# Window attention in a fused two-block kernel: the addition of the projection's bias to a strip's input moves from VectorE to GpSimd

## The reference

```
x = x + window_attention(layernorm(x))      # 8x8 shifted windows, 8 heads of 16
t = t + routed_ffn(layernorm(t))            # the upper half of the tokens by a score
x = x + conv3x3(layernorm(x), quantized)
t = t + experts(layernorm(t))               # gates from a graph attention over 524288 edges
```

## Time and profile before

| | before |
|---|---|
| median of 3 runs | 10792.27 us (10772.9 to 10792.55) |
| the profiled execution's own time | 10787.32 us |
| its span, first to last instruction | 10785.5 us |
| mean granted TensorE clock | 0.732 of 2.4 GHz |
| attention, 1059 to 3141 us | 2082 us: DVE busy 1937.69, ACT 1755.59, PE 1590.78, POOL 1088.21 |
| the moved addition on DVE | 56 instructions, 70.5 us |

### The profile page before, as it was taken

How to read it: one execution, slowest core, us unless ns; L and a number is a source line. 1 busy time by engine, 2 the same in 40 slices (tenths; PEclk the granted TensorE clock), 3 DMA queues, 4 the chain that set the end, 5 groups by cost and what they waited for, 6 DMA issues and landing times. The chain is left out here.

```text
span 10785.5 us, 111540 instructions
## 1 busy us (share of the span) xinstructions
PE 4563.0 (42%) x31813; PEld 2715.7 (25%) x31813; DVE 5474.9 (51%) x14162; ACT 3929.5 (36%) x9657; POOL 6184.6 (57%) x6259
## 2 busy tenths in 40 slices
PE   0011777777758997873222222223223223223000
PEld 0011555555544444541111111111111101101000
DVE  9987999999986775541121121121121112112487
ACT  0011888888854554332121111112112112112255
POOL 0000555555532224667777777777777777777675
PEclk9755999999978998876666666666666666666555
DMA  0000111111121223543222222222222222222366
GB/s 20 2 0 34 40 39 38 39 41 38 39 78 55 62 62 100 141 121 55 44 46 49 44 46 49 44 42 53 44 42 53 44 42 53 44 42 48 134 250 244
DMA packets 1326096, 663.81 MB, mean 62 GB/s; under 512 B 1058255, under 2 KB 1239100, under 8 KB 1320764
## 3 DMA queue, kind: packets, MB, share of 16 engines
q1 hardware_dynamic: 1142396, 576.49, 19.5%
q0 software_dynamic: 183104, 80.22, 5.7%
HBM read 344.86 MB, written 313.71 MB: 61 GB/s over the span
## 5 line engine op out<-in xcount | busy, mean ns | idle before, releaser
L1832 POOL DMA_INDIRECT gr_rec<-rec,gr_idx x4096 | 3954.2, 965 | 1248.8 <-issue 1248.0
L1853 PE MATMUL gr_p_h<-gr_tT,gr_w 128*128 128x512 f32 x1568 | 849.4, 696 | 3671.7 <-ACT gr_hT L1887 3638.7
L1972 DVE TENSOR_SCALAR gr_pen<-gr_same 128x64 f32<-128x64 f32 x64 | 13.7, 213 | 3170.6 <-DMA gr_rec<-rec,gr_idx 3170.6
L1853 PEld LDWEIGHTS gr_p_h<-gr_tT,gr_w 128*128 128x128 f32 x1568 | 347.6, 227 | 4154.9 <-ACT gr_hT L1887 3723.8
L544 POOL TENSOR_TENSOR at_sq<-at_qk 128x256 f32<-128x256 f32 x392 | 290.2, 740 | 1844.1 <-ACT at_qk L594 1843.9
L1900 ACT ACTIVATE gr_ee<-gr_dd 128x512 f32<-128x512 f32 x64 | 40.3, 629 | 3588.0 <-DVE gr_dd L1991 3588.0
L1858 PE MATMUL gr_p_y<-gr_hT,gr_w 128*128 128x512 f32 x1568 | 688.9, 592 | 0.0
L1952 DVE STREAM_TRANSPOSE gr_z<-gr_yb 128x2048 f32<-128x2048 f32 x98 | 226.5, 2311 | 902.8 <-issue 491.5
L1887 ACT ACTIVATE gr_hT<-gr_p_h,gr_b 128x512 f32<-128x512 f32 x784 | 517.6, 688 | 191.7 <-PE gr_p_h L1853 191.0
L2140 POOL DMA_INDIRECT cb_a<-scan,cb_idx x392 | 499.0, 1273 | 133.7 <-issue 122.4
L1340 POOL DMA_INDIRECT adst<-co_rec,co_idx x448 | 424.5, 948 | 223.3 <-issue 123.1
(11 more groups left out here) (358 smaller groups left out, 13212.1 us busy)
## 6 DMA issues: line engine op xcount, KB each, us to landing
y<-gr_z SPq DMA_DIRECT2D x392, 256.0 KB, 5.4
cb_y<-y SPq DMA_DIRECT2D x28, 3584.0 KB, 13.2
gr_rec<-rec,gr_idx POOLq DMA_INDIRECT x4096, 2.3
scan<-gr_out SPq DMA_DIRECT2D x64, 768.0 KB, 3.8
at_xs<-in_x_win SPq DMA_DIRECT2D x56, 448.0 KB, 3.8
x<-at_x SPq DMA_DIRECT2D x56, 448.0 KB, 4.2
ff_x<-x SPq DMA_DIRECT2D x56, 448.0 KB, 3.4
x<-ff_x SPq DMA_DIRECT2D x784, 32.0 KB
```

Source lines behind the costliest of these rows:

```text
L1832: nc.gpsimd.indirect_dma_start(out=rec[s][:, j, :], out_offset=None, in_=rec_dram, in_offset=bass.IndirectOffsetOnAxis(ap=idx[s][:, j:j + ...
L1853: nc.tensor.matmul(p_h[m % 4][:, :], w1[:, P * m:P * (m + 1)], tT[b.k][:, :], start=True, stop=True).then_inc(S["hp"], 1)
```

## The change

The definition of `residual` and its two calls go from DVE's program to POOL's. On POOL it is called once ahead of the steps and then at j = 3, behind `sq`. It gets the waits that DVE had implicitly: for the load of `xs`, and for the last reading of the `xb` buffer by `x1`. DVE waits for `xb` before the `x1` of a strip's first pair.

```
             @block.gpsimd
             def _(pool):
+                def residual(s, strip):
+                    pool.wait_ge(S[f"x_in{s}"], (strip // 2 + 1) * 16)
+                    be = beff[:, :].rearrange("p (o c) -> p o c", o=1).to_broadcast([P, PPS, C])
+                    nc.gpsimd.tensor_tensor(xb[s][:, :, :], xs[s][:, :, :], be, ALU.add).then_inc(S["xb"], 1)
+
+                pool.wait_ge(S["setup"], 6)
+                residual(0, 0)
+
                 def emit(p):
                     if p.has(3):
...
                         nc.gpsimd.tensor_tensor(sq[r][:, :], qk[r][:, :], qk[r][:, :], ALU.mult).then_inc(S["sq"], 1)
+                    strip, s, j = p.strip(0)
+                    if j == 3 and p.has(0) and p.has(PPS):
+                        p.wait("x1", -4)
+                        residual(1 - s, strip + 1)
...
-                def residual(s):
-                    be = beff[:, :].rearrange("p (o c) -> p o c", o=1).to_broadcast([P, PPS, C])
-                    nc.vector.tensor_tensor(xb[s][:, :, :], xs[s][:, :, :], be, ALU.add).then_inc(S["xb"], 1)
...
                     if p.u == -4 and p.first:
                         stats(0, 0)
-                        residual(0)
...
                         stats(1 - s, strip + 1)
-                    if j == 3 and p.has(0) and p.has(PPS):
-                        residual(1 - s)
...
                         p.wait("proj", -3)
+                        if j == 0:
+                            v.wait_ge(S["xb"], strip + 1)
```

## The result

The changed kernel takes 10825.82 us (median of 6 runs, 10812.86 to 10837.6) against 10790.72 (6 runs, 10772.9 to 10792.55) in the same measurement: a ratio of 1.0036, 95% interval 1.0023 to 1.0049. That is 35 us slower; the forecast was 35 us slower.

What follows compares the result with a forecast made beforehand. DVE's queue was taken to bound attention. Losses of 27.6 and 8.6 us less 1.1 gave +35 on the profiled 10787.3, so 10822; adding 5 to reach the median gave 10827 us. Range 10775 to 10862, own case 10812 to 10850.

Steps and rivals of the forecast that it cites:

- What bounds: In attention, DVE's own queue sets the length (busy 1937.7 of 2082 us), and POOL has room.
- The exclusion and its order: POOL's addition blocks DVE's two-SBUF-input instructions for 2.08 us; whichever engine waited already goes ahead of the other's next instruction.
- Case (a): Step j = 3, `sq` before `qkn`: POOL's addition goes ahead of `es_junk`; loss 0.89 us in 31 strips, 27.6 us.
- Case (b): Step j = 3, `sq` behind `qkn`, gathered data there: `es_junk` goes first, `es_i` is held; -0.07 us in 16 strips.
- The rival that small instructions pass: 128x7 instructions pass POOL's running addition, only `junk` is held: -0.70 us a strip; mechanism of the faster rival, chance 0.13.
- Case (c): Step j = 3, `sq` behind `qkn`, data late: the addition precedes `es_junk`; loss 1.08 us in 8 strips, 8.6 us.
- Sum: Over the strips: 27.6 + 8.6 - 1.1, total +35 us.
- The dearer rival: Addition gets ahead of `qkn`, delaying `kn`, scores and next `lg`: 1.5 to 2 us a strip, near 10885; chance 0.11.
- The faster rival: POOL's addition is hidden: -38 us (10754), or all 60 us (10732) if nothing on DVE is held; chance 0.13.
- The 5.9 us wait at the start: While the pipeline fills, DVE waits for `rs` anyway, so the first strip's addition counts as nothing.
- the SP queue: No DMA moves to another queue; SP's load still waits for `xb` of a strip before.
- the new wait of DVE for `xb`: Before `x1`, never the last wait fulfilled: one instruction hidden while `oT` runs, else at most 0.05 us, 3 in all.

Runs made afterwards that it cites:

- experiment 2: Kernel before, its addition kept on DVE, plus a useless one of the same shape and inputs on POOL: 10897.54 us against 10788.7, ratio 1.0105.
- experiment 1: Kernel before with 54 of 56 additions left out on either engine (output not the reference's): 10768.6 us against 10788.7, ratio 0.9983.
- experiment 3: Changed kernel with POOL's addition waiting for the x1 of the same step instead of the step before: 10785.15 us against the kernel before's 10788.7, ratio 0.9998.
- experiment 4: Changed kernel with POOL adding only four of a strip's seven pairs: 10789.84 us against the kernel before's 10788.7, ratio 1.0001.
- experiment 10: Changed kernel with a zero fill of the same tile in place of POOL's addition: 10769.99 us against the kernel before's 10791.49, ratio 0.9983.
- experiment 7: Changed kernel with POOL's addition at j = 1 instead of j = 3 and three xb buffers: 10814.49 us against the kernel before's 10786.85, ratio 1.0027.
- experiment 5: Kernel before with 54 additions left out and block_of at the end of step j = 3: 10763.47 us against 10786.85, ratio 0.9981.
- experiment 11: Changed kernel with the addition cut into seven of 128x128, one behind sq in each step: 10811.33 us against the kernel before's 10791.49, ratio 1.0019.

## Why the prediction was right, point by point

- *What bounds*: DVE's queue, confirmed for time that is added: a hold of DVE passed into the time in full (experiment 2: +109 for +106). For time that is taken away it holds in part only: 54 additions of 1.08 us less on DVE gave 20 us (experiment 1).
- *The exclusion and its order*: confirmed in the traces of the changed kernel and by experiments 2, 3, 4 and 10.
- *Case (a)*: 31 strips at +0.89 us were forecast. Found are 27 at about +0.9 (7.50 against 6.60) and 5 at +1.5 whose gathers land very late; the kernel before has two steps of that kind. The 31 were counted by the addition's duration (1.08 us, not 1.50), but in three of them `sq` came behind and was itself held, as rows 8 show in one; by order the kernel before has 28 with `sq` first. That the changed kernel has 32 was not foreseen.
- *Case (b)*: 16 strips at -0.07; found 14 at +0.15 (6.75 against 6.60). The sign was off because the instruction held is `es_c`, which has one SBUF input, and not the `es_i` behind it; I had named only those with two. The rival that small instructions pass is refuted by the same row: 1.29 us.
- *Case (c)*: 8 strips at +1.08; found 8 at +1.11.
- *Sum*: +35 forecast, +39.0 in the steps j = 3, +34.9 in the stage, +35.1 in the medians. That the last two agree so closely with the forecast is partly luck: (b) was some 3 us too low, (a) 1.4 (with the two late steps of before taken off), and the -4 of the other steps was missing.
- *The dearer rival* did happen, in 3 strips, but cost them no more than case (a) does, 7.46 us a step, since `qkn` and `es_junk` share one hold. I had priced it at 1.5 to 2 us. In j = 1, with DVE's `bn_stats` behind `qkn`, it cost more (experiment 7).
- *The faster rival* assumed that the removed 60 us were there to be had. Experiments 1 and 5, with no addition anywhere, put the prize at 20 and 23 us: the addition on DVE covered the landing of the gathers and, behind that, `oT`'s inputs. This was not in the prediction, which weighed only the exclusion.
- The 5.9 us wait at the start, the SP queue, the new wait of DVE for `xb`: no sign of a cost.

## What to carry to other kernels

Before moving an elementwise instruction from a full DVE to an idle POOL, look in the trace for DVE instructions that met a POOL one and see how long they got; if POOL's instruction reads SBUF, its whole duration has to be placed where DVE's queue needs no second access, and what may come ahead of it in DVE's queue matters as much as what follows. A fill did not hold two-input instructions, but it held two `tensor_scalar`. Then ask what the instruction covers where it is: here leaving it out for nothing was worth 20 us of its 70, since a landing and a chain over PE and ACT were ready to take its place. A wait that decides who goes first (experiment 3) can be worth as much as the move.

## What was unexpected

POOL's additions of 128, 512 and 896 columns take 446, 1260 and 2074 ns at least, a straight line of 2.12 ns a column and 0.17 us. `sq`, with 612 ns for 256 columns, lies 0.1 us below it; it multiplies a tile with itself. Whether the equal inputs or the multiplication make it cheaper was not tried. The prediction had set `sq` and 2077 ns side by side as fitting, and the expectation of experiment 11 drew the line through the two, which is why a piece of 128 columns was put at 0.32 us. A DVE instruction of only 128x7 elements with one SBUF tensor input was held up to 1855 ns by the POOL addition, as if it were a large one (170 ns otherwise).
